# Windowed attention with a gated layer on one core: row maxima from 32-row tiles of TensorE, all row sums by additions, four PSUM banks in a common pool

## What is computed

```python
xn = _layernorm(x)                                   # x: (8, 1024, 512)
# attention, 16 heads of 32:
q, k, v = (proj(W, b) for W, b in ((Wq, bq), (Wk, bk), (Wv, bv)))
scores = jnp.einsum('bhid,bhjd->bhij', q, k) / jnp.sqrt(dk)
im = jnp.arange(L) % W                               # W = 256
scores = jnp.where(im[:, None] >= im[None, :], scores, NEG_INF)
probs = jax.nn.softmax(scores, axis=-1)
attn = jnp.einsum('bhij,bhjd->bhid', probs, v)
s = attn.transpose(0, 2, 1, 3).reshape(B, L, D) @ Wo.T + bo
# gate:
w = (weights >= 0.0) * 2.0 - 1.0
g = silu(clip((xn @ w.T) * scale + bias, -100, 100))
x = x + s * g
```

## Time and profile before

| | |
|---|---|
| time, median of 3 runs | 1720.07 us (1716.95 to 1721.7) |
| span of the profiled execution | 1718.3 us |
| PE busy | 1670.7 us (97%), 11660 matmuls |
| DVE busy | 1344.2 us (78%) |
| POOL busy | 1188.0 us (69%) |
| ACT busy | 1158.4 us (67%) |

### The profile page before, as it was taken

The page is one execution under the profiler, slowest core; times in us unless marked ns, Lnnn a source line. Parts: engine busy times, 40 slices in busy tenths (PEclk is TensorE's granted clock), DMA queues, the critical chain, the costliest instruction groups (busy, mean ns, idle before and its releaser), DMA issues.

```text
span 1718.3 us, 34103 instructions
## 1 busy us (share of the span) xinstructions
PE 1670.7 (97%) x11660; PEld 781.8 (45%) x11660; DVE 1344.2 (78%) x2641; ACT 1158.4 (67%) x2734; POOL 1188.0 (69%) x1186
## 2 busy tenths in 40 slices
PE   8999999999999999999999999999999999999988
PEld 4444444444444444444444444444444444444433
DVE  6889677787778877888777877778777787777874
ACT  4577676677677765677756777666776677666763
POOL 0167667786867768777588775787757786667775
PEclk9999999999999999999999999999999999999989
DMA  7314212333123421234122331224312332122111
GB/s 212 110 39 88 69 45 63 87 89 85 34 71 92 100 57 46 68 99 100 38 63 69 104 85 37 75 63 111 76 38 64 81 99 54 42 63 75 44 51 50
DMA packets 185038, 126.09 MB, mean 73 GB/s; under 512 B 106912, under 2 KB 159264, under 8 KB 184416
## 3 DMA queue, kind: packets, MB, share of 16 engines
q1 hardware_dynamic: 183904, 123.13, 28.2%
q10 hardware_dynamic: 960, 0.79, 0.2%
HBM read 41.50 MB, written 17.05 MB: 34 GB/s over the span
## 4 chain that ended last, share of the span: by engine, by line
PE 83%; ACT 7%; DVE 5%; issue 2%; POOL 1%; DMA 1%; ACTq 0%; SPq 0%; POOLq 0%; DVEq 0%
PE pJ L496 29%; PE pO L698 15%; PE pS L655 11%; PE pT L679 10%; PE pT L675 3%; PE pJ L588 3%; PE pJ L592 3%; PE pJ L589 3%; ACT pS L808 3%; PE pS L658 3%; DVE mx L1008 2%; ACT PT L796 2%; PE pT L639 2%; PE pJ L583 1%; ACT acc L796 1%
## 5 line engine op out<-in xcount | busy, mean ns | idle before, releaser
L1008 DVE TENSOR_REDUCE mx<-pS 128x1 f32<-128x512 f32 (+3 forms) x1216 | 780.6, 656 | 258.0 <-PE pS L655 176.0
L796 ACT ACTIVATE PT<-pT 128x512 f32<-128x512 f32 (+1 forms) x1088 | 621.6, 583 | 431.1 <-PE pT L679 381.6
L1205 POOL TENSOR_TENSOR acc<-acc,PT 128x512 f32<-128x512 f32 x628 | 763.9, 1250 | 30.3 <-PE pO L698 30.3
L655 PE MATMUL pS<-QK 96*128 96x512 f16 (+3 forms) x1280 | 389.7, 318 | 20.1 <-ACT pS L808 14.5
L679 PE MATMUL pT<-QK 97*128 97x512 f16 (+3 forms) x1280 | 393.4, 318 | 4.2 <-ACT PT L796 1.6
L808 ACT ACTIVATE pS<-pS,a 128x384 f32<-128x384 f32 (+3 forms) x512 | 266.1, 524 | 13.8 <-DVE a L1023 13.4
L698 PE MATMUL pO<-PT,V 128*32 128x512 f32 (+3 forms) x2816 | 262.4, 486 | 0.2 <-ACT PT L796 0.2
L655 PEld LDWEIGHTS pS<-QK 96*128 96x128 f16 x1280 | 124.4, 98 | 166.0 <-issue 44.4
L496 PE MATMUL pJ<-xT,wh_q 128*128 128x512 f16 x512 | 191.7, 379 | 2.2 <-ACT xT L737 1.7
L496 PE MATMUL pJ<-wh_v,xT 128*128 128x512 f16 x512 | 192.5, 379 | 0.8 <-ACT V L776 0.8
L496 PE MATMUL pJ<-xT,wh_k 128*128 128x512 f16 x512 | 192.6, 381 | 0.0
(11 more groups left out here) (166 smaller groups left out, 2294.5 us busy)
## 6 DMA issues: line engine op xcount, KB each, us to landing
QK<-sg SPq DMA_DIRECT2D x756, 64.0 KB
xs<-in_x SPq DMA_DIRECT2D x60, 256.0 KB, 3.2
xr<-in_x SPq DMA_DIRECT2D x58, 256.0 KB, 3.0
out<-xr SPq DMA_DIRECT2D x58, 256.0 KB, 2.5
QK<-aT SPq DMA_DIRECT2D x256, 1.0 KB, 1.7
rq<-moved SPq DMA_DIRECT2D x132, 2.0 KB, 1.8
QK<-in_x SPq DMA_DIRECT2D x8, 256.0 KB, 4.0
QK<-in_mqk SPq DMA_DIRECT2D x2, 512.0 KB, 9.2
```

Of the source, the lines that this page charges most:

```text
L655: ins = e.matmul(s_bank("s", i)[:, base:base + wide], q4[0:96, j, qc], k4[0:96, j, 0:wide], start=True, stop=True)
L796: e.activation(probabilities_at(i), t_bank("t", i)[:, 0:cols], ACT.Exp, scale=SS).then_inc(s_p, 1)
L1008: e.tensor_reduce(mx[:, par, part, :].rearrange("p (j q) -> p j q", q=4)[:, heads[0]:heads[-1] + 1, qi], s_bank("s", i)[:, 0:cols].rearran ...
L1205: e.tensor_tensor(a, a, PT[:, RING_AT[i] % NPT, 0:width * len(heads)].rearrange("p (j q) -> p j q", j=len(heads)), ALU.add).then_inc(s_ap, 1)
```

## The change

The diff does four things.

1. Scores for the maxima are made of the high halves only, straight from the staged `sg`, 32 rows a head: four matmuls of the four heads stand on four row tiles (rows 32 j to 32 j + 31) and write four banks, pS[0 to 2] and one of the pool. In a diagonal block a second set of four adds the mask from a small constant `mk`. The work comes in 10 batches a group, of one or two blocks. DVE reduces the fourth head's bank alone and the three of pS with one instruction. A batch starts when both reductions of the batch before are done (`s_m0`).
2. The row sums of all units are made by additions, `acc` is doubled, and `sum_rows`, `row_shifts`, `move_sums` and the zero rows go.
3. `pT`, the third of three separate pS tensors and `pJ` give way to one `pS` of three banks and a pool of four: `BANK` gives each use the bank that comes free first by assumed holding times (`HELD`), and `bank_free` waits for the use before.
4. `PT` has 8 slots instead of 12, and every due time is written anew, in one table `TM`.

The core of the diff:

```diff
-NPT = 12
+NPT = 8
...
+TM = {
+    "s": ((1.66, 6.46, 13.04, 17.35, 19.17, 7.49, 28.14, 24.58, 32.18, 35.62), (5.99, 3.53, 8.33, 12.91, 33.26, 19.35, 22.39, 25.98, 29.14, 35.35), (4.21, 13.39, 8.01, 25.29, 36.85, 20.04, 18.01, 29.74, 34.59, 22.98), (9.9, 3.89, 26.29, 13.08, 21.26, 7.66, 34.29, 31.5, 17.41, 36.69)),
+    "held": (0.82, 1.57, 1.44, 1.41, 0.5, 1.22, 1.5, 1.17),
+    "pv": (1.48, 1.49, 0.06, 1.45, 1.78, 2.47),
...
+    "add": (2.82, 3.16),
...
+    for _part in range(_n % NQS + 1):
+        _diag = _part == _n % NQS
+        for _blocks in (((0, 128, 0), (1, 256, 128)), ((2, 384, 0),), ((3, 512, 0),)) if _diag else tuple(((q, 512, 0),) for q in range(4)):
+            BATCHES.append((38 * (_n // 2 - 1) + TM["s"][_n // 2 % NG][3 * (_n % NQS) + _k], (_n, _part, _diag, _blocks)))
+            _k += 1
...
+RING = [i for i, (n, kb, w, hs) in enumerate(T_TILES) if kb > 0]
...
 def by_vector(n, kb):
-    return kb >= (3 if n == NU - 1 else 4 * (n % NQS) + 2)
+    return kb >= (6 if n % NQS else 2)
...
-    return at_t(T_LAST[n, kb | 1]) + 1.44 + 0.01 * (kb & 1)
+    return at_t(T_LAST[n, kb | 1]) + TM["pv"][n % NQS * 2 + kb // 2] + 0.01 * (kb & 1)
...
+HELD = dict(zip(("t", "sm", "s", "qk", "v", "f", "o", "b"), TM["held"]))
+USES = sorted([(at_t(i), ("t", i)) for i in range(len(T_TILES))] + [(at_sums(n), ("sm", n)) for n in range(NU)] +
...
+for _t, _u in USES:
+    _k = min(range(4), key=lambda k: _until[k])
+    BANK[_u], BEFORE[_u] = _k, _user[_k]
+    _until[_k], _user[_k] = max(_t, _until[_k]) + LEN.get(_u[0], 0) + HELD[_u[0]], _u
...
             def scores():
...
+                    ln.wait_ge(s_m0, TAKEN[i])
+                    ln.wait_ge(*bank_free("s", i))
+                    to = [pS[:, 0, :], pS[:, 1, :], pS[:, 2, :], bank("s", i)[:, :]]
+                    for qi, w, c0 in blocks:
+                        q0, k0 = 512 * qs + P * qi, 512 * part
+                        for j in range(4):
+                            r = slice(32 * j, 32 * j + 32)
+                            ins = e.matmul(to[j][:, c0:c0 + w], sg[r, 0, q0:q0 + P], sg[r, 2, k0:k0 + w],
+                                           start=True, stop=not diag)
+                        if diag:
+                            for j in range(4):
+                                r = slice(32 * j, 32 * j + 32)
+                                ins = e.matmul(to[j][:, c0 + w - P:c0 + w], mk[r, 0, :], mk[r, 1, :], start=False, stop=True)
                     ins.then_inc(s_S, 1)
...
+                    for qi, w, c0 in blocks:
+                        e.tensor_reduce(mx[:, par, part, 12 + qi:13 + qi], bank("s", i)[:, c0:c0 + w], AX.X,
+                                        ALU.max).then_inc(s_m3, 1)
+                    yield at_s(i) + TM["mx"][1]
+                    for qi, w, c0 in blocks:
+                        e.tensor_reduce(mx[:, par, part, :].rearrange("p (j q) -> p j q", q=4)[:, 0:3, qi],
+                                        pS[:, :, c0:c0 + w], AX.X, ALU.max).then_inc(s_m0, 1)
...
                 for k, i in enumerate(ADD_V):
                     n, kb, width, heads = T_TILES[i]
-                    yield at_t(i) + 8.11
+                    yield at_t(i) + TM["add"][1]
```

More of the change, by code:

```diff
@@ L213, in at_gate @@
     first = past("f", *divmod(i, NT)) + 0.5
-    return first + (0, -0.45, 2, 4.84, 5.5)[k] / 5.5 * min(4.65, past_o(i) + 0.3 - first)
+    return first + TM["gate"][k] / 5.5 * min(4.65, past_o(i) + 0.3 - first)
 def at_ln_first(i):
@@ L289, in build @@
         V = sb("V", [P, NSLOT, NT, P], F32)
-        acc = sb("acc", [P, 4, 512], F32)
+        acc = [sb(f"acc{i}", [P, 4, 512], F32) for i in range(2)]
         PT = sb("PT", [P, NPT, 512], F32)
@@ L355, in build @@
         s_y2, s_y3, s_th, s_u, s_f = sm("s_y2"), sm("s_y3"), sm("s_th"), sm("s_u"), sm("s_f")
-        moved = [nc.dram_tensor(f"moved{i}", (P, 16), F32, kind="Internal").ap() for i in range(2)]
         x_view = x.rearrange("b (w t r) d -> b t r w d", w=4, t=NT)
@@ L636, in row_sums @@
                     ln.wait_ge(s_av, adds_v(n))
-                    ln.wait_ge(*t_bank_free("sm", n))
+                    ln.wait_ge(*bank_free("sm", n))
                     for j in range(4):
-                        ins = e.matmul(t_bank("sm", n)[32 * j:32 * j + 32, :], ones[:, :], acc[:, j, :],
+                        ins = e.matmul(bank("sm", n)[32 * j:32 * j + 32, :], ones[:, :], acc[n % 2][:, j, :],
                                        start=True, stop=True)
@@ L643, in scores @@
             def scores():
-                for i, (m, qi, part, width, heads) in enumerate(S_TILES):
+                for i, (m, part, diag, blocks) in enumerate(S_TILES):
                     yield at_s(i)
                     gn, qs = divmod(m, NQS)
-                    q4, k4 = QK[gn % 2][:, 0, qs], QK[gn % 2][:, 1, part]
-                    qc = slice(qi * P, qi * P + P)
-                    for half in range(qs + 1):
-                        ln.wait_ge(*placed(gn, half))
-                    ln.wait_ge(*s_bank_free("s", i))
-                    for k, j in enumerate(heads):
-                        base, wide = k * width, width if part < qs else width - P
-                        if wide > 0:
-                            ins = e.matmul(s_bank("s", i)[:, base:base + wide], q4[0:96, j, qc], k4[0:96, j, 0:wide],
-                                           start=True, stop=True)
-                        if wide < width:
-                            ins = e.matmul(s_bank("s", i)[:, base + wide:base + width], q4[:, j, qc], k4[:, j, qc],
-                                           start=True, stop=True)
+                    ln.wait_ge(s_msk, 16)
+                    ln.wait_ge(s_xl, NT)
+                    ln.wait_ge(s_qh, 4 * gn + 2 + qs + (part and 1))
+                    ln.wait_ge(s_m0, TAKEN[i])
[11 more added lines that the diff above has]
+                                ins = e.matmul(to[j][:, c0 + w - P:c0 + w], mk[r, 0, :], mk[r, 1, :], start=False, stop=True)
                     ins.then_inc(s_S, 1)
@@ L665, in scores_t @@
                     gn, qs = divmod(n, NQS)
-                    slot = t_bank("t", i)
+                    slot = bank("t", i)
                     q4, k4 = QK[gn % 2][:, 0, qs], QK[gn % 2][:, 1, kb // 4]
                     kc = slice(kb % 4 * P, kb % 4 * P + P)
+                    ln.wait_ge(*placed(gn, qs))
+                    ln.wait_ge(*placed(gn, kb // 4))
                     ln.wait_ge(s_cd[n % 2], 64 * (n // 2 + 1))
-                    ln.wait_ge(*t_bank_free("t", i))
+                    ln.wait_ge(*bank_free("t", i))
                     for k, j in enumerate(heads):
@@ L887, in output_bias @@
                 ln.wait_ge(s_bp, 1)
-                e.tensor_tensor(Y[:, :], bank("b", 0)[:, :], bob[:, :], ALU.add).then_inc(s_br, 1)
+                e.tensor_tensor(Y[:, :], bank("b", 0, 0)[:, :], bob[:, :], ALU.add).then_inc(s_br, 1)
                 ln.wait_ge(s_br, 1)
@@ L1199, in additions @@
                     n, kb, width, heads = T_TILES[i]
[L1200 to L1201 removed]
+                    yield at_t(i) + TM["add"][0]
+                    a = acc[n % 2][:, heads[0]:heads[-1] + 1, 512 - width:512]
                     ln.wait_ge(s_pv, units(n) + 1)
```

355 lines of the change are left out of this document (130 added, 225 removed), and 11 rows, old and new, of the table TM.

## The result

The changed kernel takes 1800.11 us (median of 4 runs, 1799.23 to 1801.59) against 1718.61 us before (4 runs): a ratio of 1.047, with a 95% interval of 1.0454 to 1.0487. It is slower, and the time lies above the whole range. The profiled execution spans 1797.4 us, 79.1 more than before.

What follows compares the result with a forecast made beforehand. The prediction took the columns that PE streams as the bound: 1718.3 - 122 + 33 + 8 = 1637 us, + 45 of stalls = 1682, or 1684 us as median of runs. The range went from 1630 to 1765 us.

Steps and rivals of the forecast that it cites:

- Part 1: PE's scores for maxima: four 32-row tiles run at once, 8.05 to 4.25 us a group, gain 122 us.
- Part 2: Row sums by addition: PE +33 us; ACT falls to 774 us; POOL's and DVE's new adds lie beside PE's work.
- (c): Row tiles on PE overlap less than column tiles: half +36, 1720 us, chance 0.11; whole 73 us, 1757, chance 0.05.
- (d): Row tiles on PE run one after the other: 1923 us; chance 0.04.
- Rival (b): DVE stands at its odd-unit adds for POOL's twenty, some 3.5 us a group: +64 us, 1748 us; chance 0.22.
- Part 4: Single pS and pool of four: PE stalls 24 us at pS and 21 us at T tiles, together 45 us.
- The forecast of the span: Whole kernel: 1637 us of PE's work plus 45 of stalls, 1682 us; as median of runs 1684 us.
- the 8 of the tail: Kernel's end: the last unit's adds, sum, transposes and reciprocal finish at about 1715, some 8 us behind.
- Part 3: DVE's wider reductions: 38 to 24 instructions a group, 733 us in all against 784, -51; DVE ends at 1333 us.
- Part 5: Order and ring: PT from 12 to 8 slots taken as 0; the last unit's end some 8 us behind.
- The prediction's last sentence: POOL's adds beside a busier DVE: if they lengthen, (b) and the ring of eight get worse than priced.

Runs made afterwards that it cites:

- no_even_adds: Changed kernel with the additions of kb 1 to 3 of every even unit left out: 1740.45 us.
- dve_late: Changed kernel with DVE's additions of odd units (all but the last) due 8.11 tiles behind their T tile instead of 3.16: 1757.3 us.
- no_adds: Changed kernel without any additions, so that the row sums hold kb 0 alone: 1666.84 us.
- tail_on_pe: dve_late with even units' kb 2 and kb 3 summed by PE straight from PT instead of added by DVE, sum 0.5 tiles earlier: 1734.44 us.
- raw_even: Changed kernel with even units' outputs copied out of pO by ACT and the copy multiplied by R on DVE afterwards: 1786.47 us.
- late_raw: Changed kernel with the edits of both dve_late and raw_even: 1769.07 us.
- short_max: Changed kernel with DVE's three-bank reduce reading only the first quarter of the columns: 1774.25 us.
- even_pool: dve_late with the even unit's three last additions moved from DVE to POOL, which makes all seven: 1906.03 us.
- late_no_even: dve_late with all additions of the even units left out: 1706.5 us.
- early_pv: dve_late with the even unit's first two PVs 1.42 tiles earlier in the order, the row sums kept in place: 1780.82 us.

## Why the prediction was wrong

**Part 1 (row tiles) was right.** The start distances show 4 ns between the heads, 0.22 a set and 0.10 a door; PE's work fell by 81.8 us where parts 1 and 2 had 89. Rivals (c) and (d) are out. The estimate of 43 us in (c) took 0.067 us as a fixed price of each of 20 sets a group; with the columns it would be some 23 us.

**Part 2 (sums by addition) is the step that failed**, in its last sentence: "POOL's and DVE's new adds lie beside PE's work as long as their queues keep up". They do not lie beside it. no_even_adds prices those of the even units at 59.7 us, and dve_late the early place of DVE's odd ones at 42.8; all additions, old and new, are 133 (no_adds). The busy time was nearly right (POOL 1344 us, predicted 1329; DVE 1418, predicted 1333), and it was the wrong thing to look at. The additions of the even unit are links in a chain of engines, each in its own order: first PV, POOL, DVE, sum on PE; and R, multiply, `pO` free and the next first PV close it to a loop. Shown is the part up to the sum: with DVE's link taken out, the sums' stall is 3.4 us instead of 54.6 (tail_on_pe). Not shown is that the loop as a whole sets the pace: cut at `pO`, the time falls by 13.6 us (raw_even) or rises by 12 (late_raw). Before, the sums of even units came from ACT's exponentials of pS, from which nothing led back to `pO`'s accumulation, and the odd unit had 8.11 tiles for its part. The prediction costed 128 of POOL's and 95 of DVE's new additions by their durations and asked who had time; it did not ask what waits for the sum. That question is answered in the diff: the sum waits for `s_ap` and `s_av`, and the even unit's multiply waits for the sum.

**Rival (b)** was a true mechanism. DVE stands for POOL's twenty additions for 63.3 us in 32 times (predicted 3.5 us in each of 32 groups, 112), and putting the additions back to 8.11 tiles gives 42.8 us (predicted 64). The time it gave, 1748, was the nearest of all, but by its mechanism alone it would have been 1684 + 43. The loss at the even sums comes on top, and is priced by tail_on_pe: 51 us of stall, 22.9 us of time after the 20 us that the replacement costs on PE.

**Part 4 (45 us of stalls at single pS and pool) was right in size.** Batches and T tiles together stand 92.9 us against 55.9, 37 more. I compared with a kernel in which I took these for nearly zero; they were 55.9 already, in the head and the tail for the most part: between 200 and 1600 us all stalls of the kernel before come to 24, those of the changed one to 132. But short_max and no_adds show that these 37 hang on DVE's load as much as on the gaps that I counted: 23.5 us of the batches' 45.3 go with shorter reductions, 14.6 with the additions. So that 45 and 37 lie close is in part luck.

**What no part has**: projections (+26 us) and PVs (+13.5), which stand behind the late pieces in PE's list, the half clock (+29), and the 7 us between the heads. The forecast of the span was 1682; to it come 55 + 26 + 13.5 + 29 + 7 = 130.5, and off it 45 - 37 = 8 and the 8 of the tail, which is contained in the measured stalls: 1796.5, and measured were 1797.4. dve_late takes 16.3 of the 26 and 20.8 of the 29 away, so most of these were echoes of DVE's wait.

**Part 3** was right for the reductions (718 us for L1000 and L1004 together, predicted 733). DVE's total missed by 85: 55 is the longer addition (192 times 1.005 less 0.717), 30 the conversion L1019 (64 of 0.57 us; I had 0.2). ACT is at 919 where I had 774: I subtracted busy times of groups that overlap in the record. It mattered for nothing.

**Part 5**: the ring of eight costs 12.6 us in the kernel before and no more than single runs differ by in the changed one (4.3, against an eleven-slot ring); taken as 0. In the last unit POOL's twenty additions took 26.2 us (1754.54 to 1780.69) and DVE's three 4.4 instead of 2.1:

```profile
1780.73 4.41 DVE L1035 TENSOR_TENSOR acc<-acc,PT 128x512 f32<-128x512 f32 x3 [5.21 <-POOL acc L1158]
...
1785.29 1.06 PE L644 MATMUL pJ<-acc,ones 128*32 128x512 f32 x8 [1.03 <-DVE acc L1035]
```

The range was too narrow because its upper end took one slow mechanism at a time, each priced by what it adds to a busy engine. even_pool shows how little that bounds: 149 us for three pieces more in each group.

**What stays open.** tail_on_pe is still 67.6 us above no_adds: 20 are the work on PE, 38.4 are stalls at batches and T tiles, 7.0 the half clock. Why the odd units' additions hold those was not taken apart further; late_no_even, 39.7 above no_adds, has 26.5 of the same kind. early_pv's loss of 23.5 us against dve_late shows T tiles (+15.1) and was not explained beyond that, nor was the rise of 12 us in late_raw.

## What to carry to other kernels

When work moves to engines that have time to spare, ask who waits for its last piece and what that releases. Where a chain of engines ends in a piece for which the busiest engine stands in its list, the sum of the links counts and not the engines' shares, and a link that can only start when another engine's last piece is done (here DVE's three additions behind POOL's four) is worth taking out even at a price on the busiest engine: with 20 us more of PE's work the time fell by 23. Stalls of PE also cost clock: with 132 us more of standing, 29 us more went to half speed.

## What the hardware showed beyond that

**Two engines at SBUF.** DVE's addition of two fp32 operands from SBUF (512 columns) takes 0.682 us where no POOL instruction lies beside it (62 of them) and 1.159 on average beside one (130): 0.69 beside a piece of 4 columns, up to 1.74 beside one of POOL's 512-column instructions, and once 2.96 beside two. In the timelines: three in 2.15 us while POOL made pieces of 4 columns, three in 4.41 us while it added results (1780.65 2.49, x2). POOL is held up as well. Its pieces of 4 columns beside DVE's additions of 881.36:

```profile
881.43 0.68 POOL L1127 TENSOR_TENSOR rs<-rs 128x4 f32<-128x4 f32 x1 [0.51 <-DVE rs L962]
882.19 0.65 POOL L1129 TENSOR_TENSOR rs<-rs 128x4 f32<-128x4 f32 x1
...
883.92 0.20 POOL L1127 TENSOR_TENSOR rs<-rs 128x4 f32<-128x4 f32 x1
```

The third row, with no DVE addition beside it, takes 0.20 us. POOL's own 512-column additions took 1.332 us on average (1.306 in the kernel before). The reductions, which read PSUM, did not stretch (1.748 us on average beside a busy POOL). The Trainium skill, SBUF — State Buffer (SBUF: two separate sides), tells of a port pair that DVE with two SBUF inputs and GpSimd lock in turn, each for a whole instruction; the 0.682 and 1.159 of DVE and the 0.20 and 0.68 of POOL agree with that. The prediction's last sentence asked whether POOL's additions would lengthen beside a busier DVE: those of 512 columns did by 0.03 us, and DVE's by 0.29 (0.717 to 1.005).
